# State-space layers of a conditioned four-layer network: the order of work inside a batch laid out anew

## The reference, cut to what matters

```python
xn = layernorm(x) * (1 + scale) + shift          # per token, D = 256
x_in, z = split(xn @ in_proj)                    # 2 x [512 tokens, 512 channels]
u = silu(causal_conv4(x_in) + conv_b)            # 4 taps per channel
dt_r, B, C = split(u @ x_proj)                   # 64, 16, 16 columns
dt = softplus(dt_r @ dt_proj + dt_b)
for t in tokens:                                 # h: [512 channels, 16 states]
    h = h * exp(dt[t] * A) + (dt[t] * u[t]) * B[t]
    y[t] = sum over states of h * C[t]
y = (y + u * D) * silu(z)
out = x + gate * (y @ out_proj)
```

## Time and profile before

| what | value |
|---|---|
| median of 3 runs | 3138.68 us (3132.44 to 3150.77) |
| the profiled execution | 3141.71 us |
| its span, first to last instruction | 3140.0 us |
| granted TensorE clock, mean | 0.91 |
| instructions | 43803 |
| busiest engines | PE 79%, DVE 70%, ACT 70%, POOL 57% of the span |
| layer 1, first scan to last multiplication by C | about 382 to 1300 us |
| layer 3, the same | about 2120 to 3098 us |

### The profile page before, as it was taken

The page is one execution under the profiler, slowest core; times in us unless marked ns, Lnnn a source line. Parts: engine busy times, 40 slices in busy tenths (PEclk is TensorE's granted clock), DMA queues, the critical chain, the costliest instruction groups (busy, mean ns, idle before and its releaser), DMA issues. The chain is left out here.

```text
span 3140.0 us, 43803 instructions
## 1 busy us (share of the span) xinstructions
PE 2479.9 (79%) x14276; PEld 1685.0 (54%) x14276; DVE 2199.4 (70%) x2822; ACT 2210.1 (70%) x3641; POOL 1787.2 (57%) x1413
## 2 busy tenths in 40 slices
PE   7787478888888888638898998848877778877885
PEld 4555256667667667512333333225665666656674
DVE  4443379778779788556776777428888778788883
ACT  2333499898898999514665666638987888878992
POOL 0000289879878889640111111027888878888895
PEclk9989699999989999867998999969999999999997
DMA  3000211101111011154555544021112112111111
GB/s 110 27 27 21 72 35 56 56 35 64 51 40 63 35 50 56 53 98 49 82 82 83 83 76 76 21 72 35 51 40 67 60 35 73 41 66 56 48 63 49
DMA packets 106136, 177.18 MB, mean 56 GB/s; under 512 B 10709, under 2 KB 91405, under 8 KB 97199
## 3 DMA queue, kind: packets, MB, share of 16 engines
q1 hardware_dynamic: 101679, 161.69, 20.0%
q0 software_dynamic: 4224, 12.59, 1.3%
HBM read 139.70 MB, written 34.14 MB: 55 GB/s over the span
## 5 line engine op out<-in xcount | busy, mean ns | idle before, releaser
L1068 POOL TENSOR_TENSOR l_h<-l_h,l_c_all 128x512 f32<-128x512 f32 x1024 | 1380.7, 1366 | 267.0 <-DVE l_h L990 251.0
L990 DVE TENSOR_TENSOR_SCAN l_h<-l_dA,l_ps_dbu 128x512 f32<-128x512 f32 x1024 | 1212.9, 1209 | 339.5 <-ACT l_dA L880 169.7
L1243 PE MATMUL l_ps_dbu<-ident,l_dub 128*128 128x128 f32 x4096 | 652.1, 284 | 230.6 <-ACT l_dub L866 152.3
L866 ACT ACTIVATE l_dub<-l_duT,l_b_tok 128x512 f32<-128x512 f32 x1024 | 727.4, 715 | 83.3 <-PE l_ps_dbu L1243 75.6
L880 ACT ACTIVATE l_dA<-l_dt,l_a_neg 128x512 f32<-128x512 f32 x1024 | 728.4, 715 | 0.2
L1218 PE MATMUL l_ps_y<-ident,l_h 128*128 128x128 f32 x4096 | 643.2, 281 | 26.8 <-POOL l_h L1068 22.3
L1243 PEld LDWEIGHTS l_ps_dbu<-ident,l_dub 128*128 128x128 f32 x4096 | 487.4, 145 | 288.6 <-DVE l_h L990 150.3
L1218 PEld LDWEIGHTS l_ps_y<-ident,l_h 128*128 128x128 f32 x4096 | 501.8, 146 | 167.3 <-issue 94.5
L1733 ACT ACTIVATE l_probs<-l_ring 128x512 f32<-128x512 f32 x512 | 293.1, 598 | 264.1 <-PE l_ring L1871 262.8
L1552 DVE TENSOR_REDUCE l_q_max<-l_ring 128x1 f32<-128x512 f32 x512 | 338.6, 683 | 177.9 <-PE l_ring L1864 176.8
L1871 PE MATMUL l_ring<-l_qs,l_ks 102*128 102x512 bf16 x512 | 202.3, 399 | 59.9 <-DMA l_qs<-l_m_parts 49.3
(11 more groups left out here) (246 smaller groups left out, 3056.2 us busy)
## 6 DMA issues: line engine op xcount, KB each, us to landing
l_c_all<-c_rows_dram SPq DMA_DIRECT2D x64, 1024.0 KB, 4.8
l_res<-x_dram SPq DMA_DIRECT2D x24, 512.0 KB, 5.6
parts_dram<-l_parts SPq DMA_DIRECT2D x48, 256.0 KB, 2.9
l_qs<-parts_dram SPq DMA_DIRECT2D x48, 256.0 KB
l_ks<-parts_dram SPq DMA_DIRECT2D x48, 256.0 KB
l_x_in<-x_dram SPq DMA_DIRECT2D x16, 512.0 KB, 5.8
x_dram<-l_res SPq DMA_DIRECT2D x16, 512.0 KB, 2.9
l_x_in<-in_x SPq DMA_DIRECT2D x8, 512.0 KB, 4.2
```

The source lines that it names most:

```text
L866: return act.activation(dub[:, n % 2, t, :], duT[:, p, t, :], ACT.Copy, scale=b_tok[:, p, t, n:n + 1])
L990: dve.tensor_tensor_scan(h[:, h_slot(s), :], dA[:, s % DA_RING, :], ps_dbu[:, dbu_slot(s), :], 0.0, ALU.mult, ALU.add).then_inc(scan_ok, 1)
L1068: pool.tensor_tensor(h[:, h_slot(s), :], h[:, h_slot(s), :], c_all[:, (n // C_GROUP) % 2, n % C_GROUP, :], ALU.mult).then_inc(hc_ok, 1)
L1243: last = pe.transpose(ps_dbu[:, dbu_slot(s), t * P:(t + 1) * P], dub[:, n % 2, t, j * P:(j + 1) * P], ident[:])
```

## The change

The same values are computed, some on another engine, and most at other units. Step by step, with the new units:

- Normalisation runs two batches ahead. In the body of b, for b+2: DVE statistics at 25, 26 and 27; ACT rstd and its negative at 31; POOL `shift` at 32, now a tensor_tensor; ACT applies it at 36 and 37; PE turns x at 52 and 54; ACT modulates at 53 and 55. SP's load of x is issued first in the body, L3's gathers move to 6, 8, 10 and 12.
- z runs one batch ahead: PE at 44, 46, 48 and 50, ACT at 45, 47, 49 and 51. In the opening the four tiles of batch 0 have banks of their own.
- Taps at 9 to 24, in_proj at 1, 4, 7 and 10, its evictions at 3, 6, 9 and 12; SiLUs at 28; x_proj at 30 and 31, x_dbl at 33.
- softplus: DVE evicts v from PSUM (tensor_scalar, 36 to 42), ACT takes |v| from SBUF.
- u*D is no longer computed on POOL. PE multiplies the u tile by a diagonal matrix of D, built once per layer, into the same place of ps_y: 16 plain products in place of 16 transposes.
- The first state's dub tiles are scaled at units 60 to 63 of the batch before.
- Post work: y turned at 13 to 19, out_proj at 21 to 26, output gate at 24 and 28, residual at 34 and 37 (L3: gathers at 40 to 43, additions at 53 and 58); SP stores y ahead of the next batch's first C load.

The diff, cut to its core:

```diff
+            if use == "z":
+                return (ps_dbu[:, 2, :], misc[:], ps_dbu[:, 0, :], ps_dbu[:, 1, :])[i]
...
+                    act.wait_ge(ln_step, b * 2 + 1)
+                    act.activation(rstd[:], rstd[:], ACT.Exp, scale=-0.5).then_inc(ln_step, 1)
+                    act.wait_ge(ln_step, b * 2 + 2)
+                    act.activation(neg_rstd[:], rstd[:], ACT.Copy, scale=-1.0).then_inc(rstd_ok, 1)
+
+                def ln_apply(b, part):
+                    if part == 0:
+                        act.wait_ge(shift_ok, b + 1)
+                    for t in (2 * part, 2 * part + 1):
                         last = act.activation(x_in[:, t, :], x_in[:, t, :], ACT.Identity, scale=rstd[:, t:t + 1], bias=shift[:, t:t + 1])
...
-                def dt_raw(b, j):
-                    act.wait_ge(dt_mm, b * JB + j + 1)
-                    act.activation(dt_in[:, j, :], bank(b, "dt", j), ACT.Identity, bias=vec(vecs, L + "_dt_b")[:, j:j + 1])
-                    act.activation(work[:, j, :], bank(b, "dt", j), ACT.Abs, bias=vec(vecs, L + "_dt_b")[:, j:j + 1]).then_inc(dti_ok, 1)
+                def softplus_abs(b, j):
+                    act.wait_ge(dtr_ok, b * JB + j + 1)
+                    act.activation(work[:, j, :], dt_in[:, j, :], ACT.Abs).then_inc(dti_ok, 1)
...
-                    if s == 3: ln_rstd(b)
-                    if s == 6: ln_apply(b)
-                    if s in (10, 12): mod(b, (s - 10) // 2)
-                    if s in (14, 18, 22, 26): x_part(b, (s - 14) // 4)
-                    if s == 36: xd(b, p)
-                    if s in (40, 42, 44, 46): dt_raw(b, (s - 40) // 2)
+                    if s in (3, 6, 9, 12): x_part(b, (s - 3) // 3)
+                    if s == 33: xd(b, p)
+                    if s in (40, 42, 44, 46): softplus_abs(b, (s - 40) // 2)
                     if s in (41, 43, 45, 47): softplus_exp(b, (s - 41) // 2)
                     if s in (42, 44, 46, 48): softplus_log(b, (s - 42) // 2)
+                    if first(b):
+                        if s in (13, 14, 15, 16): z_part(b, p, s - 13)
+                    elif s in (45, 47, 49, 51): z_part(b, p, (s - 45) // 2)
                     if s in (57, 59, 61, 63): du_tok(b, p, (s - 57) // 2)
 
...
+                def far_step(s, b):
+                    if s == 31: ln_rstd(b)
+                    if s in (36, 37): ln_apply(b, s - 36)
+                    if s in (53, 55): mod(b, (s - 53) // 2)
...
+                def first_rows(b, p, t):
+                    act.wait_ge(duT_ok, b * TB + t + 1)
+                    if t == 0:
+                        act.wait_ge(b_ok, b + 1)
+                        if not first(b):
+                            act.wait_ge(dbu_ok, b * UNITS - JB + CREDIT)
+                    last = scale_rows(p, 0, t)
+                    if t == TB - 1:
...
-                    act.wait_ge(duT_ok, b * TB + TB)
-                    act.wait_ge(b_ok, b + 1)
-                    act.wait_ge(dbu_ok, b * UNITS - JB + CREDIT)
-                    for t in range(TB):
-                        last = scale_rows(p, 0, t)
-                    last.then_inc(dub_ok, 1)
...
-                        if s in (1, 3, 5, 7): z_part(b, p, s // 2)
-                        if has_post and s in (16, 20, 24, 28): turned(b - 1, (s - 16) // 4)
-                        if s == 32:
+                        if has_post and s in (14, 16, 18, 20): turned(b - 1, (s - 14) // 2)
+                        if s == 28:
                             if has_prep:
                                 silu_u(b + 1)
                             silu_z(b, p)
                             act.preload_act_table_set(EXP_LN)
+                        if has_far: far_step(s, b + 2)
...
+                            if n + 1 == N: first_rows(b + 1, 1 - p, j)
...
+                for j in range(JB):
+                    last = dve.tensor_scalar(diag_d[:, j, :], ident[:], vec(vecs, L + "_D")[:, j:j + 1], None, ALU.mult)
+                last.then_inc(diag_ok, 1)
...
-                def ln_shift(b):
-                    dve.wait_ge(rstd_ok, b + 1)
-                    dve.scalar_tensor_tensor(shift[:], moments[:, :, 0], -1.0, rstd[:], ALU.mult, ALU.mult).then_inc(shift_ok, 1)
...
+                def dt_raw(b, j):
+                    dve.wait_ge(dt_mm, b * JB + j + 1)
+                    dve.tensor_scalar(dt_in[:, j, :], bank(b, "dt", j), vec(vecs, L + "_dt_b")[:, j:j + 1], None, ALU.add).then_inc(dtr_ok, 1)
...
-                    if s == 0: ln_stats_half(b)
-                    if s == 1: ln_stats(b)
-                    if s == 4: ln_shift(b)
-                    if 15 <= s < 15 + JB * TAPS: tap(b, (s - 15) // TAPS, (s - 15) % TAPS)
-                    if s == 37: b_copy(b, p)
-                    if s in (44, 46, 48, 50): softplus_sum(b, p, (s - 44) // 2)
+                    if 9 <= s < 9 + JB * TAPS: tap(b, (s - 9) // TAPS, (s - 9) % TAPS)
+                    if s == 34: b_copy(b, p)
+                    if s in (36, 38, 40, 42): dt_raw(b, (s - 36) // 2)
+                    if s in (43, 45, 47, 49): softplus_sum(b, p, (s - 43) // 2)
+
+                def far_step(s, b):
+                    if s in (25, 26): ln_stats(b, s - 25)
+                    if s == 27: ln_moments(b)
...
-                    if s in (49, 52): out_gate(b, p, (s - 49) // 3)
+                    if s in (24, 28): out_gate(b, p, (s - 24) // 4)
...
-                def skip_term(b, j):
-                    pool.wait_ge(xd_mm, b + 1)
-                    pool.wait_ge(du_ok, b * JB + j + 1)
-                    pool.sem_inc(passed_p, 1)
-                    pool.tensor_scalar(u[:, j, :], u[:, j, :], vec(vecs, L + "_D")[:, j:j + 1], None, ALU.mult).then_inc(skip_ok, 1)
+                def ln_shift(b):
+                    pool.wait_ge(rstd_ok, b + 1)
+                    pool.tensor_tensor(shift[:], moments[:, :, 0], neg_rstd[:], ALU.mult).then_inc(shift_ok, 1)
...
-                            if s == 16: next_rows(b + 2)
-                            if s in (18, 20, 22, 24): gather_x(b + 2, (s - 18) // 2)
+                            if s == 4: next_rows(b + 2)
+                            if s in (6, 8, 10, 12): gather_x(b + 2, (s - 6) // 2)
                         if gathered and has_post:
-                            if s in (56, 57, 58, 59): gather_y(b - 1, 1 - p, s - 56)
-                            if s in (62, 63): residual_rows(b - 1, s - 62)
+                            if s in (40, 41, 42, 43): gather_y(b - 1, 1 - p, s - 40)
+                            if s in (53, 58): residual_rows(b - 1, (s - 53) // 5)
                         if has_post:
-                            if not gathered and s in (51, 54): residual(b - 1, (s - 51) // 3)
+                            if not gathered and s in (34, 37): residual(b - 1, (s - 34) // 3)
+                        if has_far and s == 32: ln_shift(b + 2)
...
-                        if has_prep and s in (44, 46, 48, 50): dt_u(b + 1, 1 - p, (s - 44) // 2)
-                        if has_prep and s in (52, 53, 54, 55): skip_term(b + 1, s - 52)
+                        if has_prep and s in (43, 45, 47, 49): dt_u(b + 1, 1 - p, (s - 43) // 2)
...
-                    if s in (9, 11): xn_half(b, (s - 9) // 2)
-                    if s in (12, 16, 20, 24): in_proj(b, (s - 12) // 4, after_post)
-                    if s in (34, 35): x_proj(b, s - 34, after_post)
-                    if s == 37: b_turn(b, p)
-                    if s in (39, 41, 43, 45): dt_proj(b, p, (s - 39) // 2)
-                    if s in (56, 58, 60, 62): du_turn(b, (s - 56) // 2, after_post)
...
+                    if s in (1, 4, 7, 10): in_proj(b, (s - 1) // 3)
+                    if first(b):
+                        if s in (11, 12, 13, 14): z_proj(b, s - 11)
+                    elif s in (44, 46, 48, 50): z_proj(b, (s - 44) // 2)
+                    if s in (30, 31): x_proj(b, s - 30, after_post)
+                    if s == 34: b_turn(b, p)
+                    if s in (36, 38, 40, 42): dt_proj(b, p, (s - 36) // 2)
+                    if s in (56, 58, 60, 62): du_turn(b, (s - 56) // 2, before_far)
+
+                def far_step(s, b):
+                    if s in (52, 54): xn_half(b, (s - 52) // 2)
...
+                def skip_term(b, j):
+                    if not first(b):
+                        pe.wait_ge(y_ok, b * JB - JB + j + 1)
+                    elif j == 0:
+                        pe.wait_ge(diag_ok, 1)
+                    for t in range(TB):
+                        pe.matmul(ps_y[:, j, t * P:(t + 1) * P], u[:, j, t * P:(t + 1) * P], diag_d[:, j, :], start=(t == 0), stop=False,
+                                  skip_group_check=True)
...
-                        if s in (0, 2, 4, 6): z_proj(b, s // 2)
-                        if has_post and s in (14, 18, 22, 26):
-                            y_turn(b - 1, (s - 14) // 4, has_prep)
-                        if has_post and s in (47, 48, 50, 51):
```

(8 more changed lines are left out.)

148 lines of the change are left out of this document (80 added, 68 removed).

## The result

| | kernel before | kernel after |
|---|---|---|
| median of 4 runs each | 3138.64 us | 3052.18 us (3043.36 to 3053.27) |
| ratio after / before | | 0.9711, interval 0.9689 to 0.9733 |
| profiled execution, its span | 3141.7, 3140.0 us | 3052.71, 3051.0 us |
| mean granted clock of PE | 0.91 | 0.93 |

Faster, by 86 us, and inside the range; the forecast of 2995 was 57 us too low. The page's busy line, which answers to the earlier trace rows: PE has 256 more instructions (16 for each of the 16 batches), POOL lost 97 us of work, DVE 21 and ACT 49.

The account below looks back on a forecast made before the run. No engine is busy over 79%, so waits and work order bound it. Layer 1 batches: 41.9 + 10.2 + 57.5 = 109.6 us against 117.3; overall 55 + 75 + 10 + 8 + 8 - 7 = 149 us saved, forecast 2995, range 2945 to 3070.

Parts of the forecast that it names:

- no wait of 2 us at scan 0: Sign at the start of a batch: DVE no longer waits there, where it had waited 1.97 us.
- C: Last stretch of a layer 1 batch, where ACT sets the pace: 57.5 us forecast, 50.7 before.
- the wait behind the SiLUs: Sign on DVE, while ACT loads tables and does both SiLUs: down from 5.1 to 1 to 3.5 us.
- stretch B: Middle stretch of a batch, ACT's table loads and SiLUs: 10.2 us forecast, 7.4 before, with a start some 2.9 later.
- eight products at 0.62: Opening: z for the first batch costs eight products of 0.62 us, part of the 7 us added.
- "nothing" for the D products: PE's diagonal products cost the same as transposes, 275 against 273 ns, so sixteen per batch add nothing.
- A: First stretch of a batch, first scan to last convolution tap: 41.9 us forecast, 59.1 before, 1.4 left for PE waits.
- rival 1: The wait for POOL moves to first taps or softplus sums; 80 of shifts' 90 us given back, 3075 us; chance 0.16.
- the gathers of x keep their cost: Layer 3: two first taps a batch still wait 2.69 us instead of 0.54, 4.3 us a batch.
- Rival 2: PE's waits fall more and the SiLUs' late start doesn't happen: 3 us a batch, 42 us, 2950; chance 0.12.
- Rival 3: dt_raw on DVE needs POOL quiet, four times a batch: 280 us slower, 3275; chance 0.04.
- Rival 4: ACT, busiest in C, was the whole bound; only 28 us or less gained, 3110 to 3140; chance 0.06.

Follow-up runs that it names:

- run 5: Kernel after with two of the four products of every out_proj tile left out, order and waits unchanged: 3016.35 us, ratio 0.9588.
- run 6: Kernel after with the D product back on POOL (four multiplications at units 52 to 55) and PE's diagonal products made transposes again: 3078.65 us, ratio 0.9788.
- run 2: Kernel after with out_proj at units 21, 22, 27, 28 instead of 21, 22, 25, 26 and the second output gate at 29: 2984.08 us, ratio 0.9498.
- run 3: Kernel before with shift alone moved from DVE to POOL, at its old unit 4: 3146.53 us, ratio 1.0025.
- run 11: Kernel after with shift put back on DVE, at unit 33: 3044.77 us, ratio 0.9701.
- run 4: Kernel before with only the D product changed, to PE's diagonal products instead of POOL's multiplications and PE's transposes: 3093.72 us, ratio 0.9853.
- run 12: Kernel after with dt_raw, the bias addition of dt, back on ACT at units 37, 39, 41, 43: 3072.16 us, ratio 0.9788.
- run 8: Kernel after with SiLUs behind unit 27, out_proj at 21, 22, 27, 28, second gate at 29, layer 3's x gathers at 1 to 4: 2993.93 us, ratio 0.9535.

## Why the prediction was right, and where it was off

**Sign and mechanism.** Right. POOL is level with DVE in layer 1 (it has 0.1 us between a scan's end and its multiplication), the order of DVE has no 128x4 instruction, the wait at scan 0 of batch 1 is 0.8 instead of 2.0 us (in batch 3 of both layers, behind the hardware loop's jump, 3.1 are left of 4.7 and 5.8, against the sign "no wait of 2 us at scan 0"), and C came out at 57.9 for 57.5. The sign that failed in every one of the 12 batches is the wait behind the SiLUs: 4.6 to 4.8 us where 1 to 3.5 was foreseen.

**The step that failed** is in stretch B: "It starts later against the taps, by some 2.9 us". The prediction names the place, out_proj at units 25 and 26 in front of the turn of unit 27, but sizes it too small: 1.4 us before and 2.9 more make 4.3; measured are 5.8 in five batches and 7.5 in seven, together some 30 of the 55 us. The term that was mis-sized is the tiles of out_proj: one takes 1.73 us, and the prediction took half of that (the expectation of run 5 says 0.87; the prediction doesn't print it). With tiles of that half size, run 5, the SiLU of batch 1 is 4.1 us late, about as forecast; the 2.29 us in which PE stands before the gate were foreseen as a wait and can't have been far off. The hint lay in the earlier trace rows: x16 there are eight products of the code, which the prediction read as one record each in "eight products at 0.62". The other part, the half clock behind the wait (1.7 us in 7 batches, 12 us), is in no row of before. The Trainium skill (FP8 and Floating Point Precision, section TensorE Precision Notes) says that true fp32 takes four passes; no row here counts passes. This trace has two records for a plain fp32 product, 512 for 256 D products, and one for a transpose, so the earlier trace rows compared one record with one record and "nothing" for the D products was wrong: one unit's D products take 0.89 us of PE, the transposes before 0.44, and 4 x 0.45 is 1.8 us a batch. Some of it reaches DVE, as the third wait below shows.

```profile
L1259 PE MATMUL l_ps_y<-l_diag_d,l_u x512: 272/275/276, 395.5 to 2926.0; 128*128 128x128 f32 x171
```

**A's 2.2 us.** I left 1.4 us for waits on PE. Three stand in DVE's order of time of batch 1, at scans 2, 5 and 11, behind in_proj at units 1, 4 and 10, the third also behind D products:

```profile
496.16 3.44 DVE L1022 TENSOR_TENSOR_SCAN l_h<-l_dA,l_ps_dbu 128x512 f32<-128x512 f32 x3 [1.04 <-ACT l_dA L895]
500.50 1.22 DVE L1022 TENSOR_TENSOR_SCAN l_h<-l_dA,l_ps_dbu 128x512 f32<-128x512 f32 x1 [0.90 <-PE l_ps_dbu L1284]
...
511.86 1.22 DVE L1022 TENSOR_TENSOR_SCAN l_h<-l_dA,l_ps_dbu 128x512 f32<-128x512 f32 x1 [1.09 <-PE l_ps_dbu L1284]
```

Together 3.0 us; the rest of the 2.2 is spread over the sizes. The first names ACT, but that unit's dA was done at 495.0, and PE began its turn only at 495.5, behind 1.7 us of in_proj. The third is gone in run 6, where PE has no D products: 1.1 us a batch in batches 1 to 6 of layer 1 for a term that the sum had at nothing. No run moved in_proj, so the other two are read from the rows and not tested. These batches have A 2.2 us too long, one of them 3.6 (batch 4, with PE at half clock during in_proj), some 15 us of the miss. With out_proj late (run 2) layer 1 takes 766 us and layer 3 786, where the prediction's sum makes them 825.2 - 64 = 761 and 874.8 - 84 = 791. That this is close is partly luck, since A is still too long there and B shorter than forecast.

One slip in the sum itself: 149 us off the profiled 3141.7 give 2993 for a profiled execution; the median, 3.0 lower, would be 2990.

**shift.** The prediction said that it is held until POOL has caught up, and that was right; pricing it at 5.6 us each in rival 1 was not. Run 3 shows that taking it off DVE gives nothing, run 11 that putting it back costs nothing. What counts is POOL's backlog: taking the D products off POOL gives 48 us in the old order (run 4) and 26 in the new one (run 6). In layer 1 of run 6 the taps begin at unit 9, behind most of the backlog, and what is left of it is made up for by the wait at scan 11 that is gone. The move of dt_raw is worth 20 us (run 12). How the rest of the 86 us divides among z and the normalisation a batch earlier, the first state's rows and the other moves, no run separates.

**Rival 1** is half there. In the six batches of layer 3 that gather x, two taps take 2.3 to 2.9 us each, together 4.1 us a batch over those of layer 1 (4.3 forecast, "the gathers of x keep their cost"). And in six batches a softplus sum takes 5.0 to 5.9 us behind the gathers of y; that is absorbed, units 40 to 55 take 28.7 us in either layer. **Rival 2**'s 2950 asked that the late start doesn't happen; run 2 has it nearly gone, at 2984. **Rival 3** is out: dt_raw by source line is flat, at 0.73 us where 0.66 was taken.

```profile
L979 DVE TENSOR_SCALAR l_conv_in<-l_misc,vecs x56: 723/726/732, 446.0 to 2875.6; 128x512 f32<-128x512 f32 x56
```

**Rival 4** is out too: the change gave 86 us for its 28 or less, and though ACT sets the pace in C (run 12), another 65 to 68 us came from moving a single step elsewhere.

## What to carry to other kernels

When an instruction is long because it waits for a busy neighbour, price the neighbour's backlog, not the instruction: moved to that neighbour it waits in its queue, and moved to a calm place it costs nothing. In an in-order queue that feeds two others, ask of every instruction with a late input what stands behind it; here half a projection placed two units too early cost 54 us in the two stretches, 68 by the medians. And count how many records one operation of the code leaves before its duration is used in a sum.

## What the runs showed of the hardware that was not expected

- A wait of 2.2 to 2.3 us of PE is followed by half clock in some batches and by full clock in others (batches 2 and 1 of layer 1), with the same instructions around it: 0.57 to 0.67 over the next 4 us in seven batches, 1.00 in five. What decides it was not tried.
- An instruction that must have POOL quiet is held for POOL's whole unbroken run: a first tap took up to 5.74 us in run 6 and 6.62 in run 8, and all those over 2 us ended 0.3 us behind the end of POOL's run. The Trainium skill (SBUF — State Buffer, section Who interferes with whom) has the second one blocked until the first finishes; these rows exceed one multiplication (1.25 us) by far, so here it was until the run ended.
- A first tap (one tensor input in SBUF) is held as the ones with two inputs are, while dt_raw, the same kind of instruction reading PSUM, never is (0.73 us at most). That is not for want of work on POOL: 44 of its 56 began in the middle of a POOL instruction, as in batch 1 of layer 1, where the multiplication runs from 559.06 to 560.34:

```profile
559.06 1.28 POOL L1105 TENSOR_TENSOR l_h<-l_h,l_c_all 128x512 f32<-128x512 f32 x1
```

```profile
559.38 0.72 DVE L979 TENSOR_SCALAR l_conv_in<-l_misc,vecs 128x512 f32<-128x512 f32 x1
```
